# Attention rounds: the folded query in slots 2, 2, 3, 4, two score groups behind a transposition, the output product behind the turned sums

## The reference

```python
x = x + attn(layernorm(x))     # Q, K, V; softmax over causal, over 4-averaged, over top-64 scores; mean of the three; Wo
x = x + xattn(layernorm(x))    # 8 heads of 32 channels, 256 "channels" by 512 "positions" per sequence:
                               # scores = q k^T + band(rel_k); weights = softmax(scores)
                               # context = weights v + band(weights) rel_v; Wo
x = x + ffn(layernorm(x))      # expert rows picked by top-k of product keys
```

## Time and profile before

| | us |
|---|---|
| median of three runs | 2624.51 (2621.61 to 2625.58) |
| the profiled execution, its own time | 2619.07 |
| its span, first to last instruction | 2617.3 |
| busy: TensorE, VectorE, ScalarE, GpSimd | 2413.0, 2034.3, 1129.2, 1081.2 |
| a full round | 83.6 (twelve stand between 223 and 1226 us, one more up to 1310) |

### The profile page before, as it was taken

The page is one execution under the profiler, slowest core; times in us unless marked ns, Lnnn a source line. Parts: engine busy times, 40 slices in busy tenths (PEclk is TensorE's granted clock), DMA queues, the critical chain, the costliest instruction groups (busy, mean ns, idle before and its releaser), DMA issues. The chain is left out here.

```text
span 2617.3 us, 40783 instructions
## 1 busy us (share of the span) xinstructions
PE 2413.0 (92%) x12856; PEld 1332.0 (51%) x12856; DVE 2034.3 (78%) x5959; ACT 1129.2 (43%) x2623; POOL 1081.2 (41%) x1566
## 2 busy tenths in 40 slices
PE   6889999999999999999987699999999999999985
PEld 4456556565656656566554344444444444444432
DVE  1466766777676776767654289999999999999997
ACT  2256666666666666666666122222222222122210
POOL 1133333333333333333333155555555555555552
PEclk9999999999999999999999899999999999999997
DMA  3044545445554444445454599999999999999996
GB/s 109 23 124 125 161 131 151 118 143 149 157 142 128 142 139 146 125 134 161 137 144 144 200 359 384 384 385 386 387 392 385 383 382 385 383 385 382 385 374 260
DMA packets 292741, 622.47 MB, mean 238 GB/s; under 512 B 162352, under 2 KB 163376, under 8 KB 292528
## 3 DMA queue, kind: packets, MB, share of 16 engines
q0 software_dynamic: 83968, 438.34, 44.4%
q1 hardware_dynamic: 174768, 80.85, 11.5%
q10 hardware_dynamic: 33792, 100.67, 11.3%
HBM read 577.80 MB, written 142.61 MB: 275 GB/s over the span
## 5 line engine op out<-in xcount | busy, mean ns | idle before, releaser
L1103 DVE CUSTOM_DVE_ANT_0 scores<-s_bank,added 128x512 f32<-128x512 f32 x512 | 350.2, 687 | 228.8 <-PE s_bank L597 183.5
L1406 PE MATMUL l_bank<-fold,xn_tf 128*128 128x512 f32 x1024 | 452.1, 595 | 4.7 <-DMA fold<-fold_dram 2.6
L913 ACT ACTIVATE probs<-scores,nmx 128x512 f32<-128x512 f32 x512 | 373.1, 729 | 108.1 <-DVE nmx L1103 102.2
L1380 POOL DMA_INDIRECT out_rows<-rows_out,rows_now x256 | 272.2, 1063 | 353.1 <-PE out_ps L1452 284.5
L919 ACT COPY prob_t<-t_bank 128x512 f32<-128x512 f32 x512 | 299.3, 585 | 203.3 <-PE t_bank L607 202.8
L529 POOL TENSOR_TENSOR added<-mask_add,band 128x136 f32<-128x136 f32 (+1 forms) x512 | 246.9, 484 | 338.1 <-DVE nmx L1103 337.0
L1371 POOL DMA_INDIRECT in_rows<-rows_in,rows_now x256 | 310.5, 1213 | 137.3 <-DVE hid L1631 69.8
L607 PEld LDWEIGHTS t_bank<-ident,probs 128*128 128x128 f32 x2048 | 234.4, 142 | 174.7 <-issue 118.7
L1406 PEld LDWEIGHTS l_bank<-fold,xn_tf 128*128 128x128 f32 x1024 | 195.3, 191 | 250.3 <-issue 247.7
L607 PE MATMUL t_bank<-ident,probs 128*128 128x128 f32 x2048 | 316.0, 280 | 5.6 <-ACT prob_t L919 3.4
L1495 ACT COPY sims<-l_bank 128x512 f32<-128x512 f32 x128 | 74.9, 585 | 562.1 <-PE l_bank L1406 562.1
(11 more groups left out here) (188 smaller groups left out, 3715.3 us busy)
## 6 DMA issues: line engine op xcount, KB each, us to landing
rows_in<-in_in_b_dram ACTq DMA_DIRECT2D x16, 2048.0 KB, 8.8
rows_out<-in_out_a_dram ACTq DMA_DIRECT2D x16, 2048.0 KB, 9.0
rows_in<-in_in_a_dram ACTq DMA_DIRECT2D x16, 1024.0 KB, 8.2
rows_out<-in_out_b_dram ACTq DMA_DIRECT2D x16, 1024.0 KB, 5.5
rel_scratch<-rel_pad SPq DMA_DIRECT2D x16, 640.0 KB, 3.0
band<-rel_scratch SPq DMA_DIRECT2D x512, 20.0 KB, 2.3
prob_scratch<-probs SPq DMA_DIRECT2D x512, 20.0 KB, 2.2
near<-prob_scratch SPq DMA_DIRECT2D x64, 156.1 KB, 3.2
```

The source lines that it names most:

```text
L913: nc.scalar.activation(prob_tile(s % PSLOTS), scores[:, s % 2, :], ACT.Exp, bias=nmx[:, s:s + 1], scale=-1.0, accum_out=lsum[:, s:s + 1]). ...
L1103: nc.vector.tensor_tensor_reduce(out=scores[:, s % 2, :], in0=s_bank[s % HPT][:, 0:L], in1=added[:, s % 2, :], scale=-1.0, scalar=-NEG, op ...
L1380: nc.gpsimd.indirect_dma_start(out_rows[:, h, :], None, rows_out, bass.IndirectOffsetOnAxis(rows_now[:, odd, h:h + 1], 0)).then_inc(out_lo ...
L1406: ins = nc.tensor.matmul(l_bank[c % 2][:], xn_t[:, k, :], fold[:, k, c * BANK:(c + 1) * BANK], start=(k == 0), stop=(k == KD - 1))
```

## The change

Three edits, all in the order of the work; no instruction is added or removed. The products m = 0 to 3 of the folded query stand in slots 2, 2, 3, 4 instead of 2, 3, 4, 5, and ScalarE copies the pairs out in slots 2 and 4 instead of 3 and 5. The score groups of slots 16 and 20 come behind `turn` instead of ahead of it. `spread` comes ahead of `finish`, which changes slot 6 only.

```diff
-        XN, ROW_BIAS, Q, RAW, CAUSAL, MAX, E_W = 0, 0, (2, 3, 4, 5), 10, 13, 14, 17
+        XN, ROW_BIAS, Q, RAW, CAUSAL, MAX, E_W = 0, 0, (2, 2, 3, 4), 10, 13, 14, 17
...
+    SCORE_LATE = (16, 20)
...
-                if s in At.Q:
-                    m = At.Q.index(s)
+                for m in [m for m, at in enumerate(At.Q) if at == s]:
                     i, j = divmod(m, 2)
                     bank = a_open(b, "Q", i)
...
                 for s in range(STEPS):
-                    if s % HPT == 0 and cross_in_round(b):
+                    if s % HPT == 0 and s not in SCORE_LATE and cross_in_round(b):
                         score(b - 1, s, p)
                     if turn_at(b, s):
                         turn(b, s, *turn_at(b, s))
+                    if s in SCORE_LATE and cross_in_round(b):
+                        score(b - 1, s, p)
+                    if group_at(b, s, SPREAD_LAG):
+                        spread(*group_at(b, s, SPREAD_LAG))
                     if tail_in_round(b):
                         finish(b, s)
-                    if group_at(b, s, SPREAD_LAG):
-                        spread(*group_at(b, s, SPREAD_LAG))
...
                 if s in At.Q[1::2]:
-                    i = At.Q.index(s) // 2
+                    i = At.Q[1::2].index(s)
```

## The result

The changed kernel takes 2629.18 us (median of 14 runs, 2625.54 to 2634.61), the kernel before 2623.81 (14 runs, 2615.87 to 2627.58). The ratio, estimated over all executions and not the quotient of the two medians, is 1.0025, 95% interval 1.0016 to 1.0035: **slower by 0.25%**. Between the medians lie 5.4 us, just over the 5.2 us that the prediction took as the least that shows. Its profiled execution has a span of 2625.1 us against 2617.3.

A forecast was written before the change was run, and what follows sets the result against it. TensorE was taken to set the pace in full rounds. Query +10.5, round b = 1 +2.6, late groups -8.3, rounds b = 15 and 16 -1.0 sum to +3.8 us on 2624.51: 2628 us, range 2617 to 2638.

The forecast's parts named there:

- the query edit: Slots 2 to 8 of full rounds: slot 8's score group comes 0.81 us later, +10.5 us in thirteen rounds.
- the ends (b = 15 and 16): Last two attention rounds: the late score groups gain 0.5 us in each, -1.0 us together.
- The wait changed hands: Slot 6: the output product waits for `near_t` instead of `g_t`, about 1.2 us idle, and starts 0.92 us later.
- That thin cover: Slots 7 to 8: VectorE finishes slot 7 0.24 us ahead of TensorE, so its delay is just hidden.
- The late groups: Slots 16 and 20 behind `turn`: only one `turn` gained, -0.59 us a round, -8.3 us in fourteen rounds.
- the margin of `turn` 20: Slot 20: `turn` 20, waiting for `turn` 18's bank, is done 0.17 us before the score group's old start.
- rival 3: Slot 20: `turn` 20 comes late for its bank and the 0.59 gain is used up; 2636.6 us, chance 0.15.
- Round b = 1: Slot 8, without an output product: the 2.63 us delay of `e_s` arrives whole, +2.6 us.
- The bank really comes free: Slot 6: the output product waits for nothing, -1.76 us in each of thirteen rounds; 2600 us, chance 0.12.
- the bound of -1.17: Query part per full round: most it could gain, if the 1.06 us wait and `spread`'s 0.11 both went.
- Both `turn`s count: Slots 16 and 20: each full round gains 0.59 us more, giving 2620.6 us; chance 0.13.
- The clock falls: Full rounds: idle of about 1.2 us before the output product slows TensorE, some 3 us a round; 2667 us, chance 0.03.

The follow-up runs named there:

- e3_near_first: The changed kernel with `finish` ahead of `exponentials` on ScalarE: 2629.88 us against 2622.00 for the kernel before, ratio 1.0027.
- e2_late20: The kernel before with only the score group of slot 20 behind its `turn`: 2617.95 us against 2621.44, ratio 0.9982.
- e1_late: The kernel before with only the score groups of slots 16 and 20 behind `turn`: 2616.12 us against 2622.00, ratio 0.9974.
- e5_more: The kernel before with query slots 2, 3, 4, 4, `e_s`, `near_t` and output product moved earlier, slot 20 late, `spread` first: 2599.95 us against 2622.11, ratio 0.9914.
- e1_spread: The kernel before with only `spread` moved ahead of `finish`: 2619.76 us against 2622.00, ratio 0.9989.
- e2_late16: The kernel before with only the score group of slot 16 behind its `turn`: 2621.82 us against 2621.44, ratio 1.0003.
- e3_both_first: The changed kernel with `near_t` and `e_s` ahead of slot 5's exponentials on ScalarE: 2617.59 us against 2621.44 for the kernel before, ratio 0.9989.
- e2_2344: The kernel before with the folded query's products in slots 2, 3, 4, 4: 2625.53 us against 2621.44, ratio 1.0013.
- e1_query: The kernel before with only the folded query's products moved to slots 2, 2, 3, 4: 2642.30 us against 2622.00, ratio 1.0072.

## Why the prediction was right, and which terms were off

**The sum.** The prediction was 2628 us on a median of 2624.51, +3.8 us; measured were 5.4 us between the medians and 7.8 between the spans. The sign stands, the mechanism of the query edit in the full rounds stands, and the time lies in the range. Two things are luck. The thirteen full rounds were to cost 2.9 us (0.81 - 0.59 = 0.22 each) and cost 5.6, twice as much; the ends (b = 15 and 16) gave back 3.9 and not 1.0, as much more as the full rounds cost more. And of the chances, "no change" had 0.47 and "slower" 0.38: the measured difference falls just on the side that was given less.

**The query edit** was +0.81 us a round with `spread`, +0.92 without; measured +0.91 and +1.00. The third product came at t = 4.65 as replayed. The 0.09 that is missing lies right behind it, in the product's step: I took 1.83, and it is 661.90 - 659.98 = 1.92. It isn't the wait ahead of it, since the first product of a round also starts behind a wait and steps 1.83. TensorE of the kernel before, round b = 7:

```profile
647.30 1.99 PE L575 MATMUL a_bank<-xn_t,w_qk 128*128 128x256 f32 x8 [0.30 <-ACT xn_t L834]
649.13 0.60 PE L607 MATMUL t_bank<-ident,probs 128*128 128x128 f32 x4
649.57 1.89 PE L575 MATMUL a_bank<-xn_t,w_qk 128*128 128x256 f32 x8
651.39 1.14 PE L597 MATMUL s_bank<-ck,cq 32*128 32x512 f32 x8
...
656.76 1.89 PE L575 MATMUL a_bank<-xn_t,w_qk 128*128 128x256 f32 x8
658.49 0.60 PE L607 MATMUL t_bank<-ident,probs 128*128 128x128 f32 x4
```

The steps are 1.83, 1.82 and 1.73. Two things make them out. A duration of 1.99 and not 1.89 goes with 0.10 more: behind a wait or behind `weigh` the first weight load starts together with the product, behind a `turn` or PB it starts 0.11 us ahead (649.46 for the product at 649.57). And a score group behind the product costs 0.09 more than a `turn` (1.82 against 1.73). My 1.83 was the step of a product between `weigh` and a `turn`; the third product of the changed kernel has both, a wait ahead and a score group behind, 1.73 + 0.10 + 0.09 = 1.92.

After that each start is 0.05 to 0.09 later than replayed; that the output product is off by 0.05 only is chance, since `near_t` ended 0.14 later than replayed and the handoff to the product took 0.06 and not 0.15. The wait changed hands as foretold: `near_t` 0.41 and `prob_t` 0.54, 0.95 together and not 1.2; as at the third product, the idle time that the profile shows is less than what the starts lose. `rsum` came 2.76 later in its round, 14.29 for 11.53 (I had 2.63), and VectorE ended slot 7 within 0.2 us of the group of slot 8 (I had 0.24). That thin cover was real: e3_near_first fell into it.

**The late groups** were -0.59 a round; measured -0.48. The `turn` behind slot 20 gave its 0.58, the group of slot 16 nothing. The step that failed is the margin of `turn` 20: I took 0.17 us from a round in which the group of slot 20 waited 0.92 for VectorE. In ten of the thirteen rounds it waited 0.64 to 0.66, as in b = 7, and in b = 14 only 0.23; and what counts for the margin, the copy of `turn` 18 by ScalarE, ends closer to the group in all of these than in the round of the earlier trace rows. TensorE of the kernel before in b = 7, then ScalarE in b = 7 and 14 (the group of b = 14 starts at 1277.30):

```profile
692.11 1.14 PE L597 MATMUL s_bank<-ck,cq 32*128 32x512 f32 x8 [0.65 <-DVE nmx L1103]
```

```profile
690.99 0.59 ACT L919 COPY prob_t<-t_bank 128x512 f32<-128x512 f32 x1
...
1276.61 0.59 ACT L919 COPY prob_t<-t_bank 128x512 f32<-128x512 f32 x1
```

Redone with a handoff of 0.05 and with the step of 0.59 that `turn` 20 has ahead of the group in e2_late20 (691.92 - 691.33; I had taken 0.53), the group would start at 691.58 + 0.05 + 0.59 = 692.22 in b = 7, 0.11 late, and at 1277.20 + 0.05 + 0.59 = 1277.84 in b = 14, 0.54 late; in the round of the earlier trace rows 0.11 is left over. e2_late20 is 0.11 to 0.13 late by slot 20 in ten rounds, 0.55 in b = 14, and 0.01 in b = 8 and 12. In e1_late, with both groups late, it is 0.07 to 0.09, 0.50 and 0.01. So b = 14 gives back nearly all that its late group gains. By the prediction's own sign, the group of slot 20 waiting for `turn` and not for VectorE, rival 3 is what the changed kernel shows in eleven of thirteen rounds; only its price was far smaller than the 0.59 given to it. I had read one round and taken its repetition for granted ("repeat to within 0.1 us"), which is wrong by up to 0.7 between twelve of them, and by 1.4 with the last.

**Round b = 1** was to cost 2.6 and give back 0.6; the traces show +4.2. But the trace of before had a higher clock there than most: 0.91 from 140 to 160 us, as e5_more has it, and 0.83 in the ten other kernels. The same window of before and of e1_late:

```profile
140.00:160.00 20.00, 16.14 (x78) 10.69 (x79) 11.71 (x37) 8.99 (x19) 8.43 (x15) 0.91 0.25 52
```

```profile
140.00:160.00 20.00, 16.61 (x74) 10.95 (x75) 10.49 (x34) 7.73 (x18) 7.84 (x14) 0.83 0.21 43
```

e1_spread and e2_late16, whose edits give nothing in b = 1, are 2.4 and 2.2 us longer than before in that round, e1_late 1.8 with the 0.6 that it gains behind slot 20: this difference between executions is some 2.4 us. For the query edit remain about 4.2 + 0.6 - 2.4 = 2.4, near the 2.6.

The size is right, but the path was not the one that I gave. VectorE's wait for `e_s` is hardly longer there, 1.33 us for 1.04. What it waits for is the score group of slot 4, which stands behind the third product and comes late with it; VectorE of the kernel before and of the changed one, b = 1, slot 4:

```profile
158.45 0.69 DVE L1103 CUSTOM_DVE_ANT_0 scores<-s_bank,added 128x512 f32<-128x512 f32 x1 [3.06 <-PE s_bank L597]
```

```profile
163.71 0.69 DVE L1105 CUSTOM_DVE_ANT_0 scores<-s_bank,added 128x512 f32<-128x512 f32 x1 [6.67 <-PE s_bank L598]
```

The changed kernel is 3.6 us late at slot 4 already and 3.8 at slot 8, and e3_both_first, with `e_s` ahead, is still 3.4 late at slot 8 (e1_late 1.3, which is the clock). In e2_2344, where the group of slot 4 is in time, it is `e_s` that costs about as much: VectorE waits 3.06 us for it.

**In rounds b = 15 and 16** it is the other way: the changed kernel gave back 3.9 where I had 1.0. The late `turn`s are in it, and so is a clock that rose earlier; from the group of slot 20 of b = 15 to slot 0 of b = 16, in the kernel before, in the changed kernel and in e1_spread (the granted clock is the third number from the right: 0.89, 0.97 and 0.94):

```profile
1353.61:1381.50 27.89, 26.94 (x228) 18.26 (x228) 10.61 (x35) 17.44 (x42) 8.10 (x19) 0.89 0.57 174
```

```profile
1365.37:1390.65 25.28, 24.34 (x223) 16.73 (x223) 10.52 (x35) 17.43 (x42) 8.11 (x19) 0.97 0.60 191
```

```profile
1357.81:1384.46 26.65, 25.70 (x228) 17.55 (x228) 10.61 (x35) 17.45 (x42) 8.12 (x19) 0.94 0.59 182
```

Between before and the changed kernel lie 2.6 us: the `turn` that now stands ahead of the group (1.05 us at the low clock), and what follows the group at a higher clock, `weigh` 1.01 for 1.86, one product 1.82 for 2.34, and the group itself 1.83 for 2.02. The clock moves without late groups too. e1_query and e1_spread run the instructions of before in this stretch, and take 26.65 us at 0.94 for 27.88 at 0.89; e1_late has the late groups and kept 0.89, 27.24 us. So 1.2 us of difference come from the execution alone, and the late group is worth 0.6 at the same clock. Whether it can also help the clock up stays open: over b = 15 and 16 e1_late gained 0.1 us, e2_late20 1.3, e1_spread 1.6, e3_both_first 3.7.

**The rivals.** *The bank really comes free* did not happen, since ScalarE's order stood in the way; it is what e5_more made happen by moving `e_s` and the output product too, and its -0.92 us from slot 0 to 8 is inside the bound of -1.17. *Both `turn`s count* is refuted by e2_late16. *`turn` 20 comes late* holds, at 0.1 us in most rounds and 0.5 in b = 14. *The clock falls*: the full rounds kept 1.00. The waits of slot 6 in the changed kernel are two, 0.54 and 0.41, with 0.8 us of work between them, so no single idle stretch grew to the 1.2 us that I feared. Of the warning of the Trainium skill, "TensorE: Matmul & The Clock Gate", Part 1, that micro-idling between groups of matmuls may slow the clock, the full rounds show nothing: their granted clock is 1.00 in all twelve kernels.

## What to carry to other kernels

A wait is written down against the resource that came last; before moving work to free it, replay the engine that frees it, for what stood behind it in that engine's order takes its place: here moving the products cost 0.72%, while e5_more, which also moves two exponentials into ScalarE's idle time and the output product ahead of a `turn`, is 0.86% faster (late slot 20 and `spread` included). Of several waits for one slower engine, here those of slots 16 and 20, only the last gave anything, and no more than what was taken out behind it. Time each edit of a combined change alone, and read margins of a tenth of a microsecond from several rounds, not from one.

## What the runs showed of the hardware

- A product of eight passes over 256 columns has a step of 1.73 us in the full rounds, at a granted clock of 1.00, where its weights are loaded ahead. It is 0.10 more when its first weight load starts together with it, as behind a wait or behind `weigh`, and 0.09 more when a score group follows it and not a `turn`. Each step is the same in all thirteen full rounds to 0.01 us (1.73, 1.82 and 1.83 in the kernel before, 1.92 in the changed one).
- The granted clock in the start of the attention pass differs from one execution to the next, also where the program is the same up to there: e1_late differs from before in no instruction ahead of 183 us, and its clock from 140 to 160 us is 0.83 where before has 0.91. Between these two executions b = 1 differs by some 2.4 us. The Trainium skill, "TensorE: Matmul & The Clock Gate", Part 1, says that how many matmuls run slowly at a kernel's start varies from run to run. What varies here stands later, from 140 to 160 us, with 0.91 or 0.83; over the first 140 us eleven kernels have 0.96 and e5_more 0.98.
- A handoff from ScalarE to TensorE took 0.06 us (`near_t`, 669.09 to 669.15), where I had taken 0.15 from the row of `g_t`; from `prob_t` (667.33 + 0.59 = 667.92 to 667.97) it was 0.05, and from the first `g_t` to the third product (659.93 to 659.98) 0.05 too. Why the output product of before started 0.15 after `g_t` no run shows.
